# The first experts of a mixture-of-experts kernel: the order in which rows, tables and splits are asked for is changed

## The chip, the cores and the metric

The kernel runs on one core of a Trainium2 chip. The metric is the device time of one launch in microseconds (us); lower is better. The core has a matrix engine (TensorE, "PE" in the profile, with "PEld" for its weight loads), VectorE ("DVE"), ScalarE ("ACT"), GpSimd ("POOL"), and SyncE ("SP"), which here only issues transfers. Each engine works through its own list of instructions in the order in which the program gives them, and waits on counters (semaphores) that other engines and transfers raise.

## The reference

`x` is 32 x 128 x 1024 in float32, 4096 tokens of 1024. Two layers are added to it. Only the first matters here:

```
y      = each block of 128 tokens times one of 200 matrices (128 x 128)
probs  = softmax(y @ gate_w.T)                      # 64 experts
w, sel = top_k(probs, 8); w = w / sum(w)
inp[e] = the first 256 tokens that chose expert e   # a slot with no token counts as zero
h      = silu(inp[e] @ wg[e]) * (inp[e] @ wu[e])    # 1024 -> 384
out[e] = h @ wd[e]                                  # 384 -> 1024
x     += sum over a token's experts of w * out[e]
```

The second layer multiplies by a 1024 x 1024 matrix with low-rank additions; nothing in it is touched.

## The kernel before, in words

The kernel has three stages. The first (up to about 150 us) works out `y` and the routing, and stores in HBM `yd` (the rows of y), `wdr` (the routing weights), `tabd` (a table from which the tokens of each expert's slots are counted out) and `accd` (x, to which experts add). The second, which the change touches, goes through 64 experts. The third is the second layer.

**One expert on TensorE.** Weights and rows are split into a high and a low float32r part (HR and LR for weights, the two halves of XX for rows, hH and hL for h), and products are taken of the parts. `up(e)` makes three blocks, n = 3e, 3e+1, 3e+2, each of 32 matmuls (g, then u, with eight k each; lines 785 to 789), into two pairs of PSUM banks used in turn. So block n may begin only when VectorE has read block n-2: `if n >= 2: eng.wait_ge(s_gs, n - 1)`, and s_gs is raised by `join(n)`. `up(e)` also waits for the low part of all rows (`s_vl >= 2e+2`) and, unit by unit, for the weights (`s_L`). `down(e)` has 36 matmuls (line 802) in three groups j, each after hL of block 3e+j.

**A block after TensorE.** ScalarE copies half of it out (`copy_2`, L1089), VectorE adds the other half (`join`, L1522), ScalarE takes `silu` (L1093), VectorE multiplies (`product`, L1528), ScalarE rounds to hH (`high_h`, L1100), VectorE subtracts to hL (`low_h`, L1532).

**Weights.** An expert has six units of 768 KB (gA, gB, uA, uB, dA, dB), numbered through; SP loads them into four buffers `raw`. `split` is one instruction on ScalarE (HR, L1053, waiting for the load; for unit 6, which is gA of expert 1, also for stores of x) and one on VectorE (LR, L1486). The latter frees the buffer, so it releases the load of unit n+4.

**Rows.** GpSimd issues all indirect transfers, one instruction each, in a fixed order. `gather_x(e, c)` (L567) is four of them (a quarter of the columns of 128 slots each) into Xg[c]. For e >= 2 it waits for `index(e)` (s_i4) and for `turn_x(e-1, c)` (s_vt), which empties Xg[c]. `turn_x` is a VectorE transpose (L1504) from Xg[c] to XR[c]; `high_x` (ScalarE, L1081) and `low_x` (VectorE, L1510) then write XX.

**Tokens of an expert, two to three experts ahead.** `gather_tab(e)` (L542) is two transfers of 64 KB into G. `count(e)` and `token(e)` (VectorE, L1538 to L1548) wait for them and work out the slots' tokens; `spread(e)` (ScalarE, L1060 and L1064, seven small instructions) waits for `token(e)`; `index(e)` (VectorE, L1516) waits for `spread(e)`. `gather_w(e)` (L577) is two transfers of routing weights, `column(e)` (L1553) puts them in place (s_wc), `result` (ScalarE, L1107, four for one expert) scales by them, and `scatter` (L589) adds the result to accd. `gather_w(e)` waits for `column(e-2)`.

The order in which each engine does this is written out by hand: a prologue for expert 0 and the eve of expert 1, then a loop over e. In the loop, ScalarE does for e = 1: spread(3), the four results of expert 0, high_x(2, 0), high_x(2, 1), split dB 1, copy_2(3). VectorE, in the prologue: count(3), token(3), split dA 1; then in the loop turn_x(2, 0), turn_x(2, 1), index(3), low_x(2, 0), low_x(2, 1), join(3).

Of the kernel before, what the change touches and what calls it, by code (L numbers as in the profile page):

```python
# [16 lines left out]
E = 64  # L17
# [36 lines left out]
def adaln_ffn_kernel(nc, x, cond, adap, w0, gate_w, wg, wu, wd, W, A, Bm, scal,  # L54
# [14 lines left out]
    with ExitStack() as ctx:  # L69
# [437 lines left out]
        def _(eng):  # L507
# [26 lines left out]
            def gather_tab(e):  # L534
                if e == 2:
                    for s in range(4):
                        eng.wait_ge(d_ts[s], 16 * (NB // 4))
                    eng.wait_ge(s_idx, 1)
                if e >= 4:
                    eng.wait_ge(s_tok, 2 * (e - 1))  # L540
                for c in range(2):
                    eng.indirect_dma_start(G[:, e % 2, c, :], None, tab,  # L542
                                           bass.IndirectOffsetOnAxis(ap=rowi[:, c * E + e:c * E + e + 1], axis=0))\
                       .then_inc(d_g[e % 2], 16)
# [13 lines left out]
            def gather_x(e, c):  # L558
                if c == 0:
                    eng.wait_ge(s_i4, e)  # L560
                if e >= 2:
                    eng.wait_ge(s_vt, 2 * (e - 2) + c + 1)
                else:
                    eng.wait_ge(s_x0, 2 * c + 2)
                for q in range(4):
                    i = 2 * q + c
                    eng.indirect_dma_start(Xg[:, c, q, :], None, yd4,  # L567
                                           bass.IndirectOffsetOnAxis(ap=idx4[:, e % 4, i:i + 1], axis=0))\
                       .then_inc(d_xg[c], 16)

            def gather_w(e):
                if e >= 2:
                    eng.wait_ge(s_wc, e - 1)
                else:
                    eng.wait_ge(d_wy, 16 * NB // 4)
                for c in range(2):
                    eng.indirect_dma_start(Wg[:, e % 2, c, :], None, wdr,  # L577
                                           bass.IndirectOffsetOnAxis(ap=toki[:, c * E + e:c * E + e + 1], axis=0))\
                       .then_inc(d_wg[e % 2], 16)

            def scatter(e):
                if e >= 1:
                    eng.wait_ge(d_sc, 32 * e)
                else:
                    for s in range(2):
                        eng.wait_ge(d_ak[s], 16 * len(KEPT[s]))
                for c in range(2):
                    eng.wait_ge(s_out, 4 * e + 2 * c + 2)
                    eng.indirect_dma_start(acc, bass.IndirectOffsetOnAxis(ap=toki[:, c * E + e:c * E + e + 1], axis=0),  # L589
                                           ot[:, c, :], None, compute_op=ALU.add).then_inc(d_sc, 16)  # L590
# [2 lines left out]
            gather_x(1, 0)  # L593
            gather_tab(2)
            gather_x(1, 1)
            gather_tab(3)
            gather_w(0)
            gather_w(1)
            for e in range(E + 1):
                if 1 <= e < E - 3:  # L600
                    gather_tab(e + 3)
                if e >= 1:
                    scatter(e - 1)
                if e + 2 < E:
                    gather_x(e + 2, 0)
                    gather_x(e + 2, 1)
                    gather_w(e + 2)
# [346 lines left out]
        def _(eng):  # L954
# [57 lines left out]
            def store_w(i):  # L1012
                eng.wait_ge(s_wy, i + 1)
                a = i - 3
                eng.dma_start(wdr[a * P:(i + 1) * P, :].rearrange("(b q) e -> q b e", q=P),
                              wy[:, a:i + 1, :]).then_inc(d_wy, 16)
# [27 lines left out]
            def split(k, e):  # L1044
                n = pos[(k, e)]
                eng.wait_ge(d_raw[n % NRAW], 16 * (n // NRAW + 8))
                if n == 5:
                    eng.wait_ge(d_ak[0], 16 * len(KEPT[0]))
                if n == 6:
                    eng.wait_ge(d_ak[1], 16 * len(KEPT[1]))  # L1050
                if n >= NHL:
                    wait_retired(eng, n - NHL)
                eng.activation(HR[:, (n + 2) % NHL, :], raw[:, n % NRAW, :], ACT.Copy).then_inc(s_H, 1)  # L1053

            def spread(e):
                eng.wait_ge(s_tok, 2 * e + 2)
                if e >= 5:
                    eng.wait_ge(s_i4, e - 4)
                for q in range(4):
                    eng.activation(tq[0:32, e % 4, q, :], tokf[32 * q:32 * q + 32, e % 4, :], ACT.Copy)\  # L1060
                       .then_inc(s_tq, 1)
                eng.wait_ge(s_tq, 4 * e)
                for f in range(1, 4):
                    eng.activation(tq[32 * f:32 * f + 32, e % 4, :, :], tq[0:32, e % 4, :, :], ACT.Copy)\  # L1064
                       .then_inc(s_f, 1)
# [7 lines left out]
            def high_x(e, c):  # L1073
                eng.wait_ge(s_vt, 2 * (e - 1) + c + 1)
                if e == 1 and c == 0:
                    eng.wait_ge(d_wy, 16 * NB // 4)
                    for s in range(4):
                        eng.wait_ge(d_ts[s], 16 * (NB // 4))
                if e >= 2:
                    eng.wait_ge(s_up, 3 * (e - 1))  # L1080
                eng.activation(XX[:, e % 2, :, c * P:(c + 1) * P].rearrange("p j (q t) -> p q j t", q=4), XR[:, c, :, :, :],  # L1081
                               ACT.Copy).then_inc(s_vh, 1)
# [50 lines left out]
            for i in range(NB - 4, NB):  # L1133
                share(i)
            store_w(NB - 1)
            spread(1)
            split("uA", 0)
            for g in range(2):
                for c in range(2):
                    high_0(g, c)  # L1140
# [10 lines left out]
            spread(2)  # L1151
            high_x(1, 0)
            copy_2(2)
            high_x(1, 1)
            silu(2)
            high_h(2)
            for k in ("gA", "gB", "uA", "uB", "dA"):
                split(k, 1)
            for e in range(1, E):
                if e < E - 2:  # L1160
# [128 lines left out]
        def _(eng):  # L1289
# [189 lines left out]
            def split(k, e):  # L1479
                n = pos[(k, e)]  # L1480
                eng.wait_ge(s_H, n + 1)
                if n == 5:
                    eng.wait_ge(d_ak[0], 16 * len(KEPT[0]))
                if n == 6:
                    eng.wait_ge(d_ak[1], 16 * len(KEPT[1]))
                eng.tensor_tensor(LR[:, (n + 2) % NHL, :], raw[:, n % NRAW, :], HR[:, (n + 2) % NHL, :].bitcast(F32),  # L1486
                                  ALU.subtract).then_inc(s_L, 1)
# [67 lines left out]

            split("gA", 0)
            split("gB", 0)
            index(1)
            split("uA", 0)
            for g in range(2):  # L1560
                for c in range(2):
                    low_0(g, c)
# [14 lines left out]
            low_h(1)  # L1577
            turn_x(1, 0)
            index(2)
            turn_x(1, 1)  # L1580
            join(2)
            low_x(1, 0)
            product(2)
            low_h(2)
            low_x(1, 1)
            column(0)
            column(1)
            for k in ("gA", "gB", "uA", "uB"):
                split(k, 1)
            count(3)  # L1590
            token(3)
            split("dA", 1)
# [8 lines left out]
            for e in range(1, E):  # L1601
                if e < E - 1:
                    turn_x(e + 1, 0)
                    turn_x(e + 1, 1)
                    if e + 2 < E:
                        index(e + 2)
                    low_x(e + 1, 0)
                    low_x(e + 1, 1)
                join(3 * e)
                if e < E - 1:  # L1610
                    column(e + 1)
                product(3 * e)
                low_h(3 * e)
                split("dB", e)
                join(3 * e + 1)
                if e < E - 3:
                    count(e + 3)
                product(3 * e + 1)
                if e < E - 3:
                    token(e + 3)  # L1620
                low_h(3 * e + 1)
                if e + 1 < E:
                    split("gA", e + 1)
                else:
                    low_w(0)
                join(3 * e + 2)
                if e == E - 1:
                    eng.wait_ge(s_up, 3 * E)
                    eng.wait_ge(s_bh, 1)
                    eng.tensor_tensor(BL[:, :, D + NA:NX], laR[:, :, :, :].rearrange("p q a r -> p q (a r)"),  # L1630
                                      BH[:, :, D + NA:NX].bitcast(F32), ALU.subtract).then_inc(s_bl, 1)
                product(3 * e + 2)
                low_h(3 * e + 2)
                if e + 1 < E:
                    for k in ("uA", "gB", "uB", "dA"):
                        split(k, e + 1)
# [193 lines left out]
```

## Time and profile before

| what | value |
|---|---|
| median of 3 runs | 2403.81 us (2399.71 to 2403.9) |
| the profiled execution, its own time | 2391.3 us |
| its span, first to last instruction | 2389.5 us |
| busy: PE, DVE, ACT, POOL | 99%, 73%, 57%, 59% of the span |
| mean granted TensorE clock | 0.996 |

The profiled execution took 1.8 us beside its span, and was 12.5 us under the median of the runs. "Idle before" in a row is time in which that engine stood before the instruction, and the name behind it is what it waited for last. All positions are us from the span's start.

### The profile page before, as it was taken

Reading aid. Unit: us, or ns where it says so; the run is one execution under the profiler, and the core shown is the slowest. Engines: PE = TensorE matmul, PEld = TensorE weight load, DVE = VectorE, ACT = ScalarE, POOL = GpSimd, SP = SyncE. Lnnn points to the kernel's source line nnn. Section 1 sums busy time; section 2 is a strip of 40 time slices with the busy share of each in tenths; the row PEclk is TensorE's granted clock in tenths of the full one; section 3 lists DMA queues with packets and bytes.
Section 4 is the critical chain, followed back from the end, with each engine's and each line's share of the span. In section 5 each row is a group of like instructions: output and inputs, shape, how many; then the busy total and the mean of one; then the engine's idle time right before and its main releaser. Section 6 shows DMA issues by size and latency. Waiting matters only on the chain.

```text
span 2389.5 us, 35288 instructions
## 1 busy us (share of the span) xinstructions
PE 2355.3 (99%) x12762; PEld 2075.4 (87%) x12762; DVE 1734.9 (73%) x2874; ACT 1371.2 (57%) x2256; POOL 1409.5 (59%) x1032
## 2 busy tenths in 40 slices
PE   7988999999999999999999999999999999999999
PEld 5677888888888888888888888888889999999999
DVE  6887888888878878888888888887852255555554
ACT  5766777777767767777777776777751211111110
POOL 4028777787778777777777777777710132222221
PEclk9999999999999999999999999999999999999999
DMA  9998999899998998989989899899875354444441
GB/s 337 382 334 281 280 289 279 277 284 288 283 284 286 284 284 277 285 273 289 280 276 286 280 284 284 273 286 285 275 189 119 87 140 130 130 130 130 130 121 56
DMA packets 250352, 582.33 MB, mean 244 GB/s; under 512 B 82745, under 2 KB 106682, under 8 KB 250178
## 3 DMA queue, kind: packets, MB, share of 16 engines
q1 hardware_dynamic: 183202, 401.18, 51.2%
q0 software_dynamic: 55584, 160.02, 25.8%
q10 hardware_dynamic: 11392, 18.88, 2.1%
q8 instruction: 101, 1.65, 0.3%
q14 instruction: 73, 0.60, 0.1%
HBM read 456.51 MB, written 123.45 MB: 243 GB/s over the span
## 4 chain that ended last, share of the span: by engine, by line
PE 94%; DVE 1%; DMA 1%; POOL 1%; ACT 1%; issue 1%; ACTq 0%; SPq 0%; DVEq 0%; POOLq 0%
PE ps L789 26%; PE ps L802 22%; PE ps L898 16%; PE ps L788 13%; PE ps L856 5%; PE ps L785 4%; PE ps L658 2%; PE ps L891 2%; PE ps L786 2%; PE ps L668 1%; PE ps L871 1%; POOL Xg L567 1%; PE ps L681 0%; PE ps L680 0%; DMA bmR<-accd 0%
## 5 line engine op out<-in xcount | busy, mean ns | idle before, releaser
L789 PE MATMUL ps<-XX,HR 128*128 128x512 f32 x2688 | 961.6, 397 | 0.0
L788 PE MATMUL ps<-XX,LR 128*128 128x256 f32 x2688 | 751.5, 280 | 0.0
L567 POOL DMA_INDIRECT Xg<-yd,idx x504 | 654.0, 1298 | 158.5 <-issue 153.2
L1486 DVE TENSOR_TENSOR LR<-raw,HR 128x1536 fp32r<-128x1536 f32 x384 | 657.1, 1752 | 3.1 <-ACT HR L1053 3.1
L789 PEld LDWEIGHTS ps<-XX,HR 128*128 128x128 f32 x2688 | 506.2, 188 | 104.5
L1053 ACT ACTIVATE HR<-raw 128x1536 fp32r<-128x1536 f32 x384 | 556.6, 1479 | 11.9 <-DMA raw<-in_L_ffn_wd 10.3
L788 PEld LDWEIGHTS ps<-XX,LR 128*128 128x128 f32 x2688 | 508.5, 189 | 18.2 <-DVE LR L1486 0.6
L589 POOL DMA_INDIRECT accd<-ot,toki x128 | 255.9, 2000 | 159.5 <-ACT ot L1107 139.4
L898 PE MATMUL ps<-MH,xT 128*128 128x392 f32 x1536 | 335.9, 344 | 0.0
L802 PE MATMUL ps<-LR,hH 128*128 128x512 f32 x768 | 302.5, 394 | 0.0
L802 PE MATMUL ps<-HR,hL 128*128 128x512 f32 x768 | 301.1, 392 | 0.0
L802 PE MATMUL ps<-HR,hH 128*128 128x512 f32 x768 | 299.1, 389 | 1.3 <-DVE hL L1532 1.3
L898 PEld LDWEIGHTS ps<-MH,xT 128*128 128x128 f32 x1536 | 272.0, 188 | 2.3
L1522 DVE TENSOR_TENSOR gu<-ps,gu 128x512 f32<-128x512 f32 x192 | 132.7, 691 | 175.5 <-ACT gu L1089 175.5
L621 POOL DMA_INDIRECT m8a<-m8d,midx x32 | 27.7, 864 | 315.4 <-PE ps L871 314.8
L1089 ACT ACTIVATE gu<-ps 128x512 f32<-128x512 f32 x192 | 113.8, 593 | 159.4 <-PE ps L789 159.4
L542 POOL DMA_INDIRECT G<-tabd,rowi x124 | 166.2, 1340 | 39.0 <-issue 37.2
L577 POOL DMA_INDIRECT Wg<-wdr,toki x128 | 159.0, 1242 | 39.0 <-issue 38.7
L898 PE MATMUL ps<-ML,xT 128*128 128x392 f32 x768 | 181.1, 341 | 0.0
L802 PEld LDWEIGHTS ps<-HR,hL 128*128 128x128 f32 x768 | 144.2, 188 | 33.2
L802 PEld LDWEIGHTS ps<-HR,hH 128*128 128x128 f32 x768 | 144.2, 188 | 30.8 <-DVE hL L1532 1.7
L802 PEld LDWEIGHTS ps<-LR,hH 128*128 128x128 f32 x768 | 144.4, 188 | 28.7
(214 smaller groups left out, 3299.6 us busy)
## 6 DMA issues: line engine op xcount, KB each, us to landing
raw<-in_L_ffn_wd SPq DMA_DIRECT2D x128, 768.0 KB, 4.9
raw<-in_L_ffn_wg SPq DMA_DIRECT2D x126, 768.0 KB, 7.5
raw<-in_L_ffn_wu SPq DMA_DIRECT2D x126, 768.0 KB, 7.0
yd<-yrow ACTq DMA_DIRECT2D x32, 512.0 KB, 6.7
x<-accd SPq DMA_DIRECT2D x32, 512.0 KB, 5.2
out<-osb SPq DMA_DIRECT2D x31, 512.0 KB, 3.0
xt<-in_x SPq DMA_DIRECT2D x25, 512.0 KB, 8.0
accd<-xt SPq DMA_DIRECT2D x25, 512.0 KB, 6.4
```

Source lines behind the costliest of these rows:

```text
L542: eng.indirect_dma_start(G[:, e % 2, c, :], None, tab, bass.IndirectOffsetOnAxis(ap=rowi[:, c * E + e:c * E + e + 1], axis=0))\
L567: eng.indirect_dma_start(Xg[:, c, q, :], None, yd4, bass.IndirectOffsetOnAxis(ap=idx4[:, e % 4, i:i + 1], axis=0))\
L577: eng.indirect_dma_start(Wg[:, e % 2, c, :], None, wdr, bass.IndirectOffsetOnAxis(ap=toki[:, c * E + e:c * E + e + 1], axis=0))\
L589: eng.indirect_dma_start(acc, bass.IndirectOffsetOnAxis(ap=toki[:, c * E + e:c * E + e + 1], axis=0), ot[:, c, :], None, compute_op=ALU.ad ...
L788: eng.matmul(bank(out, 0, CAP), wl, xx[:, 0:CAP], start=False, stop=False)
L789: mm = eng.matmul(bank(out), wh, xx, start=False, stop=(k == 7))
L802: mm = eng.matmul(bank(4 + o), X[:, j, c * P:(c + 1) * P], Wt[:, s, j * 512:(j + 1) * 512], start=(j == 0 and m == 0), stop=(j == 2 and m ...
L856: mm = eng.matmul(bank(b0 + g, 0, z - a), X[:, j % 2, q, :], Y[:, q, a:z], start=(q == 0 and m == 0), stop=(q == 7 and m == 2))
L898: return eng.matmul(bank(lbank(t) + n, 0, 392), X[:, k, :], (MH, ML, MH)[m][:, k, a:a + 392], start=(k == 0 and m == 0), stop=(k == 7 and ...
L1053: eng.activation(HR[:, (n + 2) % NHL, :], raw[:, n % NRAW, :], ACT.Copy).then_inc(s_H, 1)
L1486: eng.tensor_tensor(LR[:, (n + 2) % NHL, :], raw[:, n % NRAW, :], HR[:, (n + 2) % NHL, :].bitcast(F32), ALU.subtract).then_inc(s_L, 1)
L1522: eng.tensor_tensor(gu[:, :, :], ps[:, b0:b0 + 2, 0:CAP], gu[:, :, :], ALU.add).then_inc(s_gs, 1)
```

## The change

It moves instructions in the prologue only, and removes and adds none.

- GpSimd: after gather_x(1, 1) the order was tab(3), w(0), w(1), x(2, 0), x(2, 1), w(2). It becomes w(0), x(2, 0), x(2, 1), tab(3), w(1), w(2). The loop then starts at e = 1 as before.
- ScalarE: split uA 0 ahead of spread(1); split gA 1 behind copy_2(2), ahead of silu(2); high_x(1, 1) behind high_h(2).
- VectorE: split uA 0 ahead of index(1); low_x(1, 0) ahead of join(2); turn_x(1, 1) behind low_h(2), then split gA 1, low_x(1, 1), the splits gB, uB and uA; column(0) behind those and ahead of count(3); column(1) between the two turns of expert 2.

```diff
--- before.py
+++ after.py
@@ -593,14 +593,16 @@
             gather_x(1, 0)
             gather_tab(2)
             gather_x(1, 1)
+            gather_w(0)
+            gather_x(2, 0)
+            gather_x(2, 1)
             gather_tab(3)
-            gather_w(0)
             gather_w(1)
-            for e in range(E + 1):
-                if 1 <= e < E - 3:
+            gather_w(2)
+            for e in range(1, E + 1):
+                if e < E - 3:
                     gather_tab(e + 3)
-                if e >= 1:
-                    scatter(e - 1)
+                scatter(e - 1)
                 if e + 2 < E:
                     gather_x(e + 2, 0)
                     gather_x(e + 2, 1)
@@ -1133,8 +1135,8 @@
             for i in range(NB - 4, NB):
                 share(i)
             store_w(NB - 1)
+            split("uA", 0)
             spread(1)
-            split("uA", 0)
             for g in range(2):
                 for c in range(2):
                     high_0(g, c)
@@ -1151,10 +1153,11 @@
             spread(2)
             high_x(1, 0)
             copy_2(2)
-            high_x(1, 1)
+            split("gA", 1)
             silu(2)
             high_h(2)
-            for k in ("gA", "gB", "uA", "uB", "dA"):
+            high_x(1, 1)
+            for k in ("gB", "uA", "uB", "dA"):
                 split(k, 1)
             for e in range(1, E):
                 if e < E - 2:
@@ -1555,8 +1558,8 @@
 
             split("gA", 0)
             split("gB", 0)
+            split("uA", 0)
             index(1)
-            split("uA", 0)
             for g in range(2):
                 for c in range(2):
                     low_0(g, c)
@@ -1577,16 +1580,16 @@
             low_h(1)
             turn_x(1, 0)
             index(2)
-            turn_x(1, 1)
+            low_x(1, 0)
             join(2)
-            low_x(1, 0)
             product(2)
             low_h(2)
+            turn_x(1, 1)
+            split("gA", 1)
             low_x(1, 1)
+            for k in ("gB", "uA", "uB"):
+                split(k, 1)
             column(0)
-            column(1)
-            for k in ("gA", "gB", "uA", "uB"):
-                split(k, 1)
             count(3)
             token(3)
             split("dA", 1)
@@ -1601,6 +1604,8 @@
             for e in range(1, E):
                 if e < E - 1:
                     turn_x(e + 1, 0)
+                    if e == 1:
+                        column(1)
                     turn_x(e + 1, 1)
                     if e + 2 < E:
                         index(e + 2)
```

## Rows read from the trace of the kernel before

**Rows 1.** The page's busy line: engine, us (share of the span), instructions.

```profile
PE 2355.3 (99%) x12762; PEld 2075.4 (87%) x12762; DVE 1734.9 (73%) x2874; ACT 1371.2 (57%) x2256; POOL 1409.5 (59%) x1032
```

**Rows 2.** TensorE waits from 150 us on: us in total, times, longest.

```profile
PE ps L785 <- DVE gu L1522: 5.2, 1, 5.2
...
PE ps L785 <- DVE XX L1493: 1.6, 1, 1.6
PE ps L802 <- DVE hL L1532: 1.3, 1, 1.3
...
PE ps L785 <- DVE LR L1486: 0.6, 1, 0.6
```

**Rows 3.** Chain that ended last, 155 to 232 us: start, us, what.

```profile
197.76 6.41 DMA Xg<-yd,idx
204.19 1.26 DVE XR L1504
...
208.41 0.70 DVE gu L1522
```

**Rows 4.** TensorE in order of time: start, us, line, operation [idle before].

```profile
209.16 0.79 PE L785 MATMUL ps<-XX,HR 128*128 128x512 f32 x1 [5.20 <-DVE gu L1522]
...
214.41 0.39 PE L785 MATMUL ps<-XX,HR 128*128 128x512 f32 x1
```

**Rows 5.** TensorE in stretches: A:B us, busy (instructions), granted clock, DMA, GB/s.

```profile
207.00:208.00 1.00, 0.00 (x0) 0.77 1.14 74
```

**Rows 6.** DVE, 148 to 245 us, in order of time; x2, x4 are merged.

```profile
159.68 1.76 DVE L1486 TENSOR_TENSOR LR<-raw,HR 128x1536 fp32r<-128x1536 f32 x1 [1.14 <-ACT HR L1053]
...
173.38 0.42 DVE L1532 TENSOR_TENSOR hL<-prod,hH 128x256 fp32r<-128x256 f32 x1 [0.48 <-ACT hH L1100]
...
181.39 0.32 DVE L1516 TENSOR_SCALAR idx<-tq,f 128x8 int32<-128x8 f32 x1
...
189.87 6.76 DVE L1486 TENSOR_TENSOR LR<-raw,HR 128x1536 fp32r<-128x1536 f32 x4
196.55 0.34 DVE L1538 TENSOR_SCALAR_CACHE_REDUCE Gj<-G,slot 128x128 f32<-128x128 f32 x1
```

**Rows 7.** ACT, 148 to 245 us, in order of time.

```profile
172.03 0.41 ACT L1093 ACTIVATE sil<-gu 128x256 f32<-128x256 f32 x1
...
182.46 0.58 ACT L1089 ACTIVATE gu<-ps 128x512 f32<-128x512 f32 x1
...
202.01 1.08 ACT L1081 ACTIVATE XX<-XR 128x1024 fp32r<-128x1024 f32 x1
205.47 1.06 ACT L1081 ACTIVATE XX<-XR 128x1024 fp32r<-128x1024 f32 x1 [2.38 <-DVE XR L1504]
```

**Rows 8.** SP's issues from 167 us.

```profile
167.27 0.96 SPq L367 DMA_DIRECT2D raw<-in_L_ffn_wg  x2
```

**Rows 9.** Transfers issued 167 to 167.6 us: count, KB each, us to landing.

```profile
raw<-in_L_ffn_wg SPq DMA_DIRECT2D x1, 768.0 KB, 16.0
```

**Rows 10.** DVE groups by shape, 180 to 210 us: busy, mean ns, idle before.

```profile
L1504 DVE STREAM_TRANSPOSE XR<-Xg 128x1024 f32<-128x1024 f32 x4 | 5.0, 1242 | 5.2 <-DMA Xg<-yd,idx 5.2
L1510 DVE TENSOR_TENSOR XX<-XR,XX 128x1024 fp32r<-128x1024 f32 x4 | 4.8, 1216 | 0.0
```

**Rows 11.** POOL, 148 to 245 us, in order of time.

```profile
179.51 0.94 POOL L542 DMA_INDIRECT G<-tabd,rowi  x1 [0.30 <-issue]
...
185.76 1.87 POOL L567 DMA_INDIRECT Xg<-yd,idx  x1 [0.30 <-issue]
...
192.75 1.36 POOL L567 DMA_INDIRECT Xg<-yd,idx  x1 [0.30 <-issue]
...
199.01 1.82 POOL L577 DMA_INDIRECT Wg<-wdr,toki  x1 [0.30 <-issue]
```

**Rows 12.** Transfers into G, 150 to 215 us: from issue to landing.

```profile
DMA to landing us min/median/max: 5.7/6.0/6.2
```

**Rows 13.** The same over the whole span, x124.

```profile
DMA to landing us min/median/max: 5.6/6.9/8.4
```

## The prediction

> **What bounds the kernel now.** I read the page first: TensorE is busy 99% of the span [rows 1], so almost only the places where it stands can be won. The list of its waits behind the routing stage gives those: 8.7 us lie around experts 0 and 1, the largest one wait of 5.2 us [rows 2]; between there and the end of expert 63 no wait of TensorE is listed. A microsecond won or lost at experts 0 and 1 therefore moves the end by a microsecond.
>
> The chain that ended last names the cause of the 5.2 us [rows 3]: the last quarter of expert 2's rows is asked for at 197.76 and lands 6.4 us later; its turn, its high and low parts and a split follow, then join(3), at 208.41. Only then may block 5 start, at 209.16; TensorE had stopped at 209.16 - 5.20 = 203.96 [rows 4]. The stall also costs clock: the granted clock falls within 207 to 208 us [rows 5], and the first 16 matmuls behind the stall take 214.41 - 209.16 = 5.25 us at the lower level (1.2 instead of 2.4 GHz), of which half, 2.6 us, is loss.
>
> The change reaches for this stall. So the question is when join(3) can run, and I follow each of its conditions.
>
> **The start (uA's split ahead of spread and index).** VectorE stood 1.14 us before this split, since ScalarE did spread(1) first [rows 6]. Now the wait goes, index(1) comes behind the split at about the time at which GpSimd is free for it anyway, and TensorE's wait of 1.6 us shrinks. Bounds 0 and 1.14 us, I take 0.6. Whether it reaches the end depends on the later stall; see the sum.
>
> **ScalarE's split gA 1 ahead of silu(2).** copy_2(2) ends at 182.46 + 0.58 = 183.04 [rows 7]. The load of gA 1 was issued at 167.27 and took 16.0 us [rows 8, 9], so it lands at 183.3: the split runs 183.3 to 184.7, and silu(2) is behind it. From silu to the end of low_h a block takes 1.77 us (172.03 to 173.38 + 0.42) [rows 6, 7], so hL is there at 186.5. TensorE waited for it until about 188.1; most of its 1.3 us goes.
>
> **VectorE's new order.** turn_x(1, 1) comes behind low_h(2): 186.5 + 1.2 = 187.7. Then split gA 1 (1.7, a quarter of the four that took 6.76) to 189.4 and low_x(1, 1) (1.2) to 190.5 [rows 6, 10]. up(1) can start at 190.6. Before, gA's split ended near 189.87 + 1.69 = 191.6 [rows 6] and set the start, so this is 1.1 us earlier. Blocks 3 and 4 are then paced by the next three splits, ending at 190.5 + 3 x 1.69 = 195.6 rather than 196.6. Block 4 ends about 202.8 instead of 203.96. So far the change gains 1.1 us, but only in reaching the next wait sooner.
>
> **GpSimd's new order.** x(2, 0) needs index(2), done at 181.7 [rows 6], so it starts at 182.0, not 185.76. x(2, 1) needs turn_x(1, 1), 187.7, and starts at 188.0. Issues follow each other every 1.25 us where nothing disturbs (0.94 + 0.30 at 179.51), every 1.66 us beside splits on VectorE (1.36 + 0.30 at 192.75), and over the eight row issues of before every (199.01 - 185.76) / 8 = 1.66 us [rows 11]. The second half of table 3 is the sixth issue from 188.0, five steps on: 6.25 us without disturbance, 8.3 by the mean. VectorE works through a split and a low part without a pause just then, and the first issues lose most behind such work, as the one at 185.76 did (1.87 us against 0.94). I take 9.5 us, so table 3's second half is asked for at 197.5 (bounds 194.2 and 198.0). In the old order it was asked for at 179.51.
>
> Expert 2's last rows now go out two issues ahead of that, at 195.0, and land near 195.0 + 6.4 = 201.4 instead of 204.2. The wait that the change attacks is therefore gained on by 2.8 us.
>
> **What is late next: table 3.** count(3) on VectorE needs both halves of it. It ran at 196.55 without any wait [rows 6]; VectorE will now reach it at about 195.7. The table's transfers take 5.7 to 6.2 us here [rows 12], 5.6 to 8.4 over the span [rows 13]. With 6.0 the table is there at 203.5, and VectorE stands almost 8 us. In its queue behind count(3) are token(3), split dA 1, both turns of expert 2, index(3), both low parts and join(3). ScalarE stands too: spread(3) waits for token(3), and behind it are the four results of expert 0, high_x(2, 0), high_x(2, 1), split dB 1 and copy_2(3), without which there is no join(3). How long this takes is in the trace: count(3) at 196.55 to high_x(2, 0) at 202.01 is 5.46 us of ScalarE working without a wait; the next high_x would have followed 1.0 us later; from high_x(2, 1) at 205.47 to TensorE at 209.16 are 3.69 us [rows 4, 6, 7]. Together 10.1 us. VectorE's own list is shorter (token, split, two turns, two low parts, about 9 us), so ScalarE's counts.
>
> Block 5 then starts at 203.5 + 0.1 + 10.1 = 213.7 instead of 209.16.
>
> The Trainium skill (DMA: Bandwidth & Descriptors, "Anatomy of one DMA — SWDGE (gpsimd) path") gives a GpSimd transfer about 2.0 us plus bytes / 436e3. Its rule would make 2.15 us of the table's 64 KB and start block 5 at 209.9, 0.7 us late only. The trace does not agree: not one of these transfers lands in under 5.6 us [rows 13].
>
> **The rest of the moves.** column(0) no longer waits and column(1) has its weights by its new place (asked for at 200.0 and 5 us on its way, needed past 207), so both cost their few tenths beside a standing engine. SP's queue: the release of gB 2's load hangs on split dA 1 and comes some 7 us later, but TensorE wants this unit only in expert 2, behind about 20 us; hidden. Expert 3's rows are behind scatter(0), which waits for the results: about 3 us later, while their need moves by 4.6 us; hidden. Clock: the stall is now 213.7 - 202.8 = 10.9 us long, the clock is down at its end as before, and I let the same 2.6 us stand (0.7 us either way).
>
> **Sum.** The 0.6 + 1.1 us won ahead of block 5 only lengthen the stall, since what ends it hangs on a landing and on GpSimd's list, not on TensorE. What counts is block 5: 213.7 - 209.16 = +4.6 us, all of which passes to the end. The profiled execution would take 2391.3 + 4.6 = 2395.9 us. The median of the runs is 12.5 us above that execution; laid on it, 2403.8 + 4.6 = 2408.4 us, +0.19%. A measurement of this kernel can tell about 0.2%, 4.8 us, from no change. Bounds of the unknown: table asked for at 194.2 and landed in 5.6 us gives block 5 at 210.0, +0.9 us; asked for at 198.0 and landed in 8.4 us gives 216.6, +7.4 us.
>
> **Rivals.**
> - *The table is late, but little.* GpSimd gets through its list at nearly 1.25 us an issue. Block 5 at 210.0 to 211.5, +0.9 to +2.3 us: 2405.5 us. For it: the issue at 179.51. Against: those beside the splits, 1.66 us and more [rows 11]. Chance 0.25.
> - *The other side: the rows decide and the stall shrinks.* Rows at 201.4 instead of 204.2 start block 5 at 206.4: -2.8 us, 2401.0 us; if the clock no longer falls, as it fell only some 4 us behind the stop [rows 5], up to 2.6 us more, 2398.4 us. It decides if the table is there by 206.4 - 10.1 = 196.3, so with 6.0 us on its way asked for by 190.3. That is 7 us ahead of what the issue rate gives. Chance 0.07.
> - *A second stall.* Expert 3's rows miss their turn, because GpSimd's list has slid and the scatter has slid into it. VectorE turned them with no wait before, and I find 1.6 us more room, so it needs an error of mine; a price of 2.5 us on top, 2410.9 us. Chance 0.08.
>
> **How the numbers follow.** My case (block 5 late by 2.5 to 7.4 us, through count(3)) has 0.60 and its own range is 2406 to 2411. The table case has 0.25, the faster one 0.07, the second stall 0.08. My case lies about the 4.8 us bound, so half of it is slower: slower 0.30 + 0.08, and a little for runs scattered upward, 0.40; same 0.52; faster 0.08. The range of 2401 to 2413 takes in both bounds, the faster rival without clock and the second stall.
>
> **What would show it.** Right: TensorE's waits list one of about 11 us at L785 for join(3); VectorE has a new wait of about 8 us for G before L1538 of count(3) at about 203.5; ScalarE stands as long before L1060; waits for Xg at L1504 vanish; the wait of 1.3 us at L802 is gone or short; up(1) begins near 190.6; no wait behind 230 us. Wrong: table 3 issued ahead of about 194 us, or G landing in 3 us, or count(3) no longer the head of both queues; or a gain ahead of block 5 that reaches the end.

## The result, and the profile after

The changed kernel takes 2406.72 us (median of 16 runs, 2403.89 to 2411.34) beside 2403.57 us (2399.71 to 2411.55) for the kernel before in the same comparison: ratio 1.0016, 95% interval 1.0009 to 1.0023. That is +3.15 us by the medians, +2.2 to +5.5 us by the interval: a little slower; the median difference is within the 0.2% that was called "same", the upper end of the interval is just beyond it. The prediction was 2408.4 us, +4.6.

The profiled execution took 2407.89 us by its own time, its span is 2406.1 us. This is 16.6 us longer than the span of before, and most of it is not the change. The first gather of expert 0's rows, which ends the routing stage, was issued at 153.14 in the profiled execution of before and is here at 164.99; in a second execution of the kernel before it is at 165.48. The 11.85 us between the two lie ahead of everything that the change moves. They go with the granted clock of the first 50 us: 1.00 in the profile of before and in the three others of this document whose first gather is at 152 to 155 us, 0.86 to 0.90 in the ten whose first gather is at 163 to 165 us. Kernels with and without the change stand in both groups. From here on I count positions from this gather and call it T0.

TensorE's waits of after from 150 us on (total, times, longest), against [rows 2]:

```profile
PE ps L787 <- DVE gu L1525: 10.8, 1, 10.8
PE ps L804 <- DVE hL L1535: 2.7, 1, 2.7
...
PE ps L787 <- DVE XX L1496: 1.0, 1, 1.0
```

The one wait of 5.2 us for join(3) has become one of 10.8. The other two went two ways: the start's from 1.6 to 1.0, that for hL from 1.3 up to 2.7. (TensorE's and ScalarE's lines stand 2 further down than before, VectorE's 3.)

TensorE of after in order of time; the first row is block 0, the second the last of the three groups of down(0), the third block 5, the last the 17th matmul of block 5, as in [rows 4]:

```profile
173.92 0.50 PE L787 MATMUL ps<-XX,HR 128*128 128x512 f32 x1 [0.98 <-DVE XX L1496]
...
199.16 0.50 PE L804 MATMUL ps<-HR,hH 128*128 128x512 f32 x1 [2.69 <-DVE hL L1535]
...
226.21 0.80 PE L787 MATMUL ps<-XX,HR 128*128 128x512 f32 x1 [10.83 <-DVE gu L1525]
...
231.19 0.39 PE L787 MATMUL ps<-XX,HR 128*128 128x512 f32 x1
```

Why join(3) is late stands on VectorE, in order of time:

```profile
202.96 5.09 DVE L1489 TENSOR_TENSOR LR<-raw,HR 128x1536 fp32r<-128x1536 f32 x3
207.96 0.16 DVE L1556 COPY wcol<-Wg 128x2 f32<-128x2 f32 x1
216.21 0.35 DVE L1541 TENSOR_SCALAR_CACHE_REDUCE Gj<-G,slot 128x128 f32<-128x128 f32 x1 [8.09 <-DMA G<-tabd,rowi]
...
225.46 0.69 DVE L1525 TENSOR_TENSOR gu<-ps,gu 128x512 f32<-128x512 f32 x1 [0.44 <-ACT gu L1091]
```

VectorE has done its splits and column(0), and then stands 8.09 us at count(3), for a table that arrives at 216.2. In [rows 6] the same instruction had no wait at all. From count(3) to block 5 are 226.21 - 216.21 = 10.0 us, the list that the prediction put at 10.1. ScalarE is empty meanwhile:

```profile
195.95 1.49 ACT L1055 ACTIVATE HR<-raw 128x1536 fp32r<-128x1536 f32 x1 [1.18 <-DMA raw<-in_L_ffn_wg]
...
217.65 0.88 ACT L1062 ACTIVATE tq<-tokf 32x2 f32<-32x2 f32 x4 [9.87 <-issue]
219.25 2.42 ACT L1109 ACTIVATE ot<-ps,wcol 128x512 f32<-128x512 f32 x4
221.55 2.02 ACT L1083 ACTIVATE XX<-XR 128x1024 fp32r<-128x1024 f32 x2
```

It stands 9.87 us ahead of spread(3); results, both high_x and copy_2(3) follow. And GpSimd shows when the table was asked for:

```profile
164.99 0.96 POOL L554 DMA_INDIRECT Xg<-yd,toki  x1 [78.80 <-DVE toki L1464]
...
193.94 0.94 POOL L567 DMA_INDIRECT Xg<-yd,idx  x1 [1.74 <-DVE idx L1519]
...
200.53 2.19 POOL L567 DMA_INDIRECT Xg<-yd,idx  x1 [1.51 <-DVE XR L1507]
203.03 2.50 POOL L567 DMA_INDIRECT Xg<-yd,idx  x1 [0.30 <-issue]
205.83 1.37 POOL L567 DMA_INDIRECT Xg<-yd,idx  x1 [0.30 <-issue]
207.50 1.37 POOL L567 DMA_INDIRECT Xg<-yd,idx  x1 [0.30 <-issue]
...
210.43 0.94 POOL L542 DMA_INDIRECT G<-tabd,rowi  x1 [0.30 <-issue]
```

x(2, 1), the rows from 200.53 on, had to wait for turn_x(1, 1), which the change put behind low_h(2); then its four issues took 7.4 us beside the splits. The table's second half went out at 210.43, T0 + 45.4; before it was T0 + 26.4 (179.51 - 153.14).

### The profile page after: what moved, and what is told of

It reads as the page before. It is cut to its first block, busy times and chain, and to the rows that moved or that the text cites. A ratio compares the mean times of both kernels' runs of the same rounds, so it can differ in the third digit from the quotient of the medians.

```text
span 2406.1 us, 35288 instructions
## 1 busy us (share of the span) xinstructions
PE 2358.3 (98%) x12762; PEld 2076.3 (86%) x12762; DVE 1735.6 (72%) x2874; ACT 1370.5 (57%) x2256; POOL 1408.0 (59%) x1032
## 4 chain that ended last, share of the span: by engine, by line
PE 95%; DMA 1%; DVE 1%; issue 1%; ACT 1%; another core or an unknown queue 0%; SPq 0%; ACTq 0%; POOL 0%; DVEq 0%; POOLq 0%
PE ps L791 25%; PE ps L804 21%; PE ps L900 17%; PE ps L790 13%; PE ps L858 5%; PE ps L787 4%; PE ps L660 2%; PE ps L893 2%; PE ps L788 2%; PE ps L670 1%; PE ps L873 1%; DMA raw<-in_L_ffn_wg 1%; PE ps L683 1%; PE ps L682 0%
```

## The experiments

All positions in this table are from T0, in us. "Rows" is the last request for expert 2's rows, "table" that for the second half of table 3.

| run | rows | table | count(3) | join(3) | down(1) | ratio to before (95%) |
|---|---|---|---|---|---|---|
| before | 44.6 | 26.4 | 43.4 | 55.3 | 64.1 | 1 |
| b_again | 43.0 | 26.3 | 43.5 | 54.6 | 62.0 | 1.0002 (0.9991, 1.0013) |
| after | 42.5 | 45.4 | 51.2 | 60.5 | 69.0 | 1.0016 (1.0009, 1.0023) |
| after_again | 42.8 | 45.7 | 51.7 | 60.9 | 70.1 | 1.0023 (1.0014, 1.0032) |
| tab_ahead | 43.4 | 26.6 | 42.2 | 54.4 | 63.6 | 0.9993 (0.9983, 1.0004) |
| count_later | 42.7 | 46.2 | 55.0 | 54.3 | 62.8 | 0.9988 (0.9977, 0.9999) |
| gp_only | 37.4 | 40.7 | 47.9 | 57.1 | 63.6 | 1.0003 (0.9993, 1.0014) |
| eng_only | 45.8 | 26.4 | 43.4 | 56.9 | 65.6 | 0.9997 (0.9988, 1.0006) |
| gp_count_later | 38.4 | 41.7 | 51.4 | 50.7 | 57.1 | 0.9982 (0.9973, 0.9991) |
| join_first | 44.6 | 26.3 | 43.4 | 46.4 | 56.8 | 0.9977 (0.9968, 0.9986) |
| join_first_again | 44.3 | 27.3 | 44.8 | 52.8 | 63.0 | 0.9987 (0.9977, 0.9997) |
| all_fixed | 45.4 | 38.0 | 44.4 | 47.4 | 57.0 | 1.0006 (0.9997, 1.0015) |
| all_fixed2 | 43.7 | 35.5 | 42.6 | 45.5 | 55.8 | 0.9984 (0.9975, 0.9993) |
| join_first2 | 44.4 | 26.0 | 43.2 | 46.2 | 56.3 | 0.9985 (0.9975, 0.9994) |

**The kernel before, again (b_again).** No edit: what one profiled execution can tell from another.

> The kernel before once more, for a second profile and for the spread. All theories: ratio 1.000, within 0.001. If the 11.9 us that the profile of the changed kernel shows more than that of before by the end of the routing stage belong to single executions and not to the change, this profile may show them too (span near 2401); if it comes out near 2389.5 again, the change would have to answer for them. In either case TensorE's wait for join(3) should be about 5 us.

The median is 2401.85 beside 2401.89 us: no difference. T0 is 165.48, so the 12 us of the routing stage belong to the execution and not to a kernel. The 5.2 us wait, though, isn't there. TensorE's rows show gaps in block 4 for which the profile names no releaser, and a lower clock right behind them, and the block ends 1.1 us after join(3) was done:

```profile
213.51 0.28 PE L788 MATMUL ps<-XX,LR 128*128 128x256 f32 x1 [0.24 <-issue]
214.97 0.39 PE L789 MATMUL ps<-XX,HR 128*128 128x512 f32 x1 [0.81 <-issue]
216.41 0.37 PE L788 MATMUL ps<-XX,LR 128*128 128x256 f32 x1 [0.70 <-issue]
```

Block 5 begins at T0 + 56.4, where it began at 56.0 in the other execution, so nearly the same microseconds are lost. Whether this is the same stall in another form isn't shown: by its rows TensorE was still in block 4 when join(3) ended. The list of waits alone is thus no safe measure; join(3)'s own position (55.3 and 54.6) is what two executions agree on, to 0.7 us, and I judge by it.

**The table asked for ahead of expert 2's rows (tab_ahead).** The change with this one thing taken back; column(1) goes behind join(3), since its weights come later.

```diff
+            gather_tab(3)
             gather_w(0)
             gather_x(2, 0)
             gather_x(2, 1)
-            gather_tab(3)
...
                     turn_x(e + 1, 0)
-                    if e == 1:
-                        column(1)
```

> The changed kernel with table 3 asked for ahead of expert 2's rows again (the weights of expert 0 and the rows behind it), and column(1) behind join(3), since its weights now come last. My theory (the table's late landing is the whole of the loss): count(3) runs without a wait near where VectorE reaches it, the rows decide, block 5 starts about 2.2 us earlier than in the kernel before and 7 us earlier than in the changed one, counted from the first rows' gather; time 2401.4 us, ratio 0.999; with a clock that stays up some 2.5 us less, ratio 0.998. Rival (the order of the splits or the gathers costs something else): ratio 1.001 as the changed kernel.

count(3) is back at 42.2 without a wait, join(3) at 54.4, some 6 us ahead of the change and 0.2 to 0.9 ahead of before. The ratio is below that of the change by 0.0023, about 5.5 us. The table's place is the whole loss, as far as the runs can tell. What it doesn't show is the gain that I had given the rows: block 5 is at T0 + 55.2, 0.8 us ahead of before and not 2.2, and VectorE again waits for them, as before.

```profile
208.90 1.24 DVE L1507 STREAM_TRANSPOSE XR<-Xg 128x1024 f32<-128x1024 f32 x1
213.91 1.25 DVE L1507 STREAM_TRANSPOSE XR<-Xg 128x1024 f32<-128x1024 f32 x1 [3.77 <-DMA Xg<-yd,idx]
218.14 0.69 DVE L1525 TENSOR_TENSOR gu<-ps,gu 128x512 f32<-128x512 f32 x1 [0.53 <-ACT gu L1091]
```

**The table late, but out of the way (count_later).** GpSimd's order stays as changed; count(3) and token(3) go behind join(3), index(3) behind low_h(3), spread(3) behind high_h(3), and column(1) behind join(3).

```diff
-            count(3)
-            token(3)
             split("dA", 1)
...
                 join(3 * e)
+                if e == 1:
+                    column(1)
+                    count(3)
+                    token(3)
...
```

> The changed kernel with everything of expert 3's table (count, token, spread, index) and column(1) moved behind join(3); GpSimd's order is that of the change, so the table is asked for as late as there. My theory: the table's late landing no longer matters, the rows of expert 2 decide and land about 2.8 us earlier than in the kernel before, so block 5 starts 2.8 us earlier than before; time 2400.8 us, ratio 0.999 (0.998 if the clock stays up); expert 3's rows are asked for some 3 us later than before and should just be in time. Rival (GpSimd's new order is bad in itself, by the transfers' traffic or by the issue rate): ratio 1.001 or more.

The table is asked for as late as in the change, at 46.2, but nothing of block 3 stands behind it: join(3) at 54.3, ratio 0.9988. Block 5 is at 55.0, 1.0 us ahead of before and not the 2.8 that I had expected of the rows. With the two runs together the cause is shown from both sides: it is neither the late table by itself nor the place of count(3), but that count(3) stands in the queue ahead of join(3) while the table is on its way.

**GpSimd's order alone (gp_only) and the two other engines' alone (eng_only).** gp_only is the kernel before with the changed order of gathers, and column(1) between the turns of expert 2; eng_only is the reverse.

```diff
-            gather_tab(3)
             gather_w(0)
-            gather_w(1)
-            for e in range(E + 1):
+            gather_x(2, 0)
+            gather_x(2, 1)
+            gather_tab(3)
+            gather_w(1)
+            gather_w(2)
+            for e in range(1, E + 1):
...
```

> The kernel before with GpSimd's new order alone, and column(1) between the turns as in the change (ahead of the splits it would stand for weights that now come last). My theory: x(2, 1) is not held by the late turn, so the table is asked for about 2 us earlier than in the changed kernel; count(3) still waits, some 5 us; block 5 starts about 2.4 us later than in the kernel before; ratio 1.001. Rival (the moves on VectorE and ScalarE make the loss): ratio 0.999, since the rows come earlier.

> The kernel before with the moves on VectorE and ScalarE alone; GpSimd keeps the old order. My theory: up(1) starts about 1 us earlier, count(3) does not wait, but expert 2's last rows are asked for about when they were (GpSimd's list is the same, and the turn that it waits for is done at about 34 to 35 us behind the first rows' gather, when x(2, 1) would not be issued before 37 to 38 anyway), so join(3) stays near 54.5 to 55.3 us behind that gather; ratio 1.000. Rival (the engines' moves make the loss): join(3) later by 2 us or more, ratio 1.001 or more.

In gp_only the rows are asked for by 37.4, 5 us ahead of the change: turn_x(1, 1) stands in its old place, so x(2, 1) is free early, and seven of its eight issues take 0.95 to 1.02 us each. The last two on GpSimd:

```profile
198.88 0.95 POOL L567 DMA_INDIRECT Xg<-yd,idx  x1 [0.30 <-issue]
200.14 1.36 POOL L567 DMA_INDIRECT Xg<-yd,idx  x1 [0.30 <-issue]
```

In spite of that join(3) is at 57.1, 1.8 to 2.5 us behind before, since count(3) waited 4.9 us for the table. The time is unchanged (1.0003). In eng_only x(2, 1) is not held by the turn, which ends at 190.3 while the first issue of x(2, 1) comes at 195.84, right behind the one before it. What is late are the issues themselves: the last two of x(2, 0) and the first of x(2, 1) fall beside a low part and splits:

```profile
190.24 2.50 POOL L567 DMA_INDIRECT Xg<-yd,idx  x1 [0.30 <-issue]
193.04 2.50 POOL L567 DMA_INDIRECT Xg<-yd,idx  x1 [0.30 <-issue]
195.84 1.36 POOL L567 DMA_INDIRECT Xg<-yd,idx  x1 [0.30 <-issue]
```

The last request is at 45.8 and join(3) at 56.9, 1.6 to 2.3 us behind before, where I had expected it to stay; its time too is not told from no change (0.9997). So each half puts join(3) back by about 2 us, which the times don't show, and together they put it back by 5 to 6. The rest beyond the two halves comes through x(2, 1), behind which GpSimd's part has put the table. Against gp_only x(2, 1) starts 1.9 us later in the change (35.5 against 33.6), as the engines' part delays turn_x(1, 1), and from its first to its last issue it takes 7.0 us instead of 3.8, as it now runs beside the splits.

**Both handicaps gone (gp_count_later).** gp_only with count(3), token(3), spread(3) and index(3) behind block 3, as in count_later.

> GpSimd's new order with the turns of the kernel before, and expert 3's table (count, token, spread, index) and column(1) behind join(3). Expert 2's last rows should be asked for near 37.4 us behind the first rows' gather, as with GpSimd's new order alone, 5 us earlier than in the changed kernel, since the turn they wait for is not moved back and fewer of the issues stand beside splits. My theory: with the table out of the way join(3) then comes at 51 to 52 us, limited by the lists and no more by rows; down(1) at 57.5 to 59. A second wait at block 8 as in all_fixed is likely and takes 1 to 3 us back; ratio 0.998. Rival (rows asked for earlier win nothing, whatever the table does): join(3) at 54 us or later, ratio 0.999 to 1.000.

Join(3) is at 50.7, 3.6 us ahead of count_later, and TensorE's wait ahead of block 5 is down to 1.8 us:

```profile
215.44 0.50 PE L787 MATMUL ps<-XX,HR 128*128 128x512 f32 x1 [1.80 <-DVE gu L1526]
```

The ratio is 0.9982, 4.3 us under before. So asking early for expert 2's rows goes with an earlier join(3), if the turn stays where it was and the table's consumers are out of the way. How much of the time is due to the rows isn't shown: count_later, with rows at 42.7 instead of 38.4, has 0.9988, and the two intervals overlap. The second wait at block 8 that I had thought likely did not come (0.35 us).

**Block 3 worked off first (join_first, join_first_again).** The kernel before, in which only the work on block 3 goes ahead of expert 2's turns, results and high parts, of none of which it needs anything.

```diff
             for e in range(1, E):
+                if e == 1:
+                    join(3)
+                    product(3)
+                    low_h(3)
                 if e < E - 1:
                     turn_x(e + 1, 0)
```

and so for copy_2(3), silu(3) and high_h(3) on ScalarE; their old places are left out for e = 1.

> The kernel before, in which for expert 1 alone block 3 is worked off at once: copy_2(3), join(3), silu, product, high_h and low_h ahead of the turns and parts of expert 2's rows, which up(2) needs only 17 us later. GpSimd's order is that of before. My theory: what holds TensorE is only that join(3) stands in both lists behind work that it does not need. Then the wait of 5 us and its clock loss of up to 2.6 us go, and down(1) starts 7 us earlier (about 55 to 57 us behind the first rows' gather instead of 62 to 64); time about 2395 us, ratio 0.997. Rival (the stall comes back at down(1), since dB's split or hL is late in turn): ratio 0.999 or more.

> join_first once more on another occasion: down(1) at about 56.8 us behind the first rows' gather, no wait of TensorE at block 5, ratio 0.9977 within 0.001. If the gain was one of that occasion, 0.999 or more.

The first time join(3) is at 46.4, the stall at block 5 is gone, and the ratio is 0.9977, 4.7 us under before. VectorE goes from join(3) over product and low part to the turns, at 202.58 and 204.77, with 0.94 us left of the wait for rows:

```profile
199.95 0.68 DVE L1528 TENSOR_TENSOR gu<-ps,gu 128x512 f32<-128x512 f32 x1
202.58 1.24 DVE L1510 STREAM_TRANSPOSE XR<-Xg 128x1024 f32<-128x1024 f32 x1
204.77 1.25 DVE L1510 STREAM_TRANSPOSE XR<-Xg 128x1024 f32<-128x1024 f32 x1 [0.94 <-DMA Xg<-yd,idx]
```

The second time the same kernel has 0.9987, and the profiled execution (2401.24 us, beside a median of 2398.38) missed both positions that I had expected: join(3) is at 52.8, block 5 had a wait of 0.79 us, and down(1) began at 63.0 instead of 56.8. It shows what the new order can cost. TensorE began up(1) 2.7 us later than in join_first, VectorE stood 4.87 us at join(3) with expert 2's turns and the split of expert 1's dB behind it, and TensorE then waited for that split:

```profile
199.84 0.50 PE L802 MATMUL ps<-HR,hH 128*128 128x512 f32 x1 [2.40 <-DVE hL L1538]
216.40 0.50 PE L785 MATMUL ps<-XX,HR 128*128 128x512 f32 x1 [0.79 <-DVE gu L1528]
...
225.88 0.80 PE L802 MATMUL ps<-HR,hH 128*128 128x512 f32 x1 [3.60 <-DVE LR L1492]
```

Why join(3) was so late is open. VectorE waited for copy_2(3) on ScalarE, which began only at 215.03, although TensorE's rows have block 4 beginning at 209.86; the profile doesn't name what released it:

```profile
215.03 0.60 ACT L1089 ACTIVATE gu<-ps 128x512 f32<-128x512 f32 x1 [6.03 <-remote]
```

**All of it together (all_fixed), and the next block too (all_fixed2, join_first2).** all_fixed is the change with block 3 worked off first, and the table between x(2, 0) and x(2, 1). all_fixed2 and join_first2 are all_fixed and join_first with block 6 also worked off early, between the turns of expert 3 on VectorE and between its high parts on ScalarE:

```diff
                 if e < E - 1:
                     turn_x(e + 1, 0)
+                    if e == 2:
+                        join(6)
+                        product(6)
+                        low_h(6)
                     turn_x(e + 1, 1)
```

> The changed kernel with the same treatment of block 3 and with table 3 asked for between the two halves of expert 2's rows, where GpSimd otherwise waits for the turn; column(1) behind the low parts. My theory: as join_first, and 1 us more since up(1) starts earlier; time about 2394 us, ratio 0.9965. Rival (up(1)'s earlier start is used up by the splits, or by transfers of gA that land late): the same as join_first.

> all_fixed, in which for expert 2 as well block 6 is worked off early, between the two turns of expert 3's rows. In all_fixed TensorE reached down(1) 7 us earlier than in the kernel before, but stood 4.3 us at block 8 for join(6), which was queued behind expert 3's last rows. My theory: that second wait and the clock it cost are all that separates all_fixed from join_first; it goes, and the ratio is 0.997 to 0.998. Rival (the second wait only moves on, to up(3), since GpSimd's list has not become shorter): ratio 0.9995 or more.

> join_first, with block 6 worked off between the two turns of expert 3's rows (as in all_fixed2). My theory: the 0.4 us that TensorE still waited at block 8 goes, and the half microsecond is too small to measure: ratio 0.9975. Rival (block 6 this early takes ScalarE's and VectorE's time away from the rows and splits of expert 3): TensorE waits at down(2) or up(3), ratio 0.9985 or more.

all_fixed gained nothing (1.0006, where I had expected 0.9965), although join(3) was at 47.4. The stall had gone one expert further on. TensorE's list of waits and VectorE's row, where expert 3's rows come late and join(6) is behind them:

```profile
PE ps L787 <- DVE gu L1531: 4.3, 1, 4.3
```

```profile
229.42 1.25 DVE L1513 STREAM_TRANSPOSE XR<-Xg 128x1024 f32<-128x1024 f32 x1 [3.21 <-DMA Xg<-yd,idx]
```

So down(2) begins at T0 + 90.7, behind the 89.1 of before. With join(6) out of the way it begins at 83.3, and all_fixed2 has 0.9984. join_first2, at 0.9985 where I had expected 0.9975, isn't told from join_first's 0.9977 and 0.9987: where the rows of expert 3 are in time, the second edit buys nothing that shows.

**The change again (after_again).** The kernel after, measured together with all_fixed2 and gp_count_later.

> The changed kernel once more, for a second profile and a second comparison. All theories: ratio 1.0016 within 0.001. If the late table is the cause, count(3) again stands about 8 us for G, join(3) comes 60 to 61 us behind the first rows' gather (55.3 and 54.6 in two profiles of the kernel before), and down(1) 67.5 to 69 us (64.1 and 62.0 before). If instead the first profile was an odd execution, join(3) is nearer to 56.

2405.32 beside 2401.03 us, 1.0023, with join(3) at 60.9, block 5 at 61.7 and a wait of 10.2 us ahead of it; down(1) is at 70.1, 1 us behind what I had expected. The mechanism is the same.

Versions faster than both kernels, each with an interval below 1, are thus join_first (0.9977 and 0.9987), gp_count_later (0.9982), all_fixed2 (0.9984), join_first2 (0.9985) and, barely, count_later (0.9988); their intervals overlap, and I can't rank them.

## Why the prediction was right

**The mechanism held, to the places.** Block 5 was put 4.6 us later; it is at T0 + 61.2 instead of T0 + 56.0, 5.2 us later. The wait was put at 10.9 us and is 10.8, VectorE's at count(3) at almost 8 and is 8.09, the list from count(3) to block 5 at 10.1 and is 10.0. tab_ahead and count_later take the effect away, each in its own way. That the length of TensorE's wait agrees to 0.1 us is partly luck: it was put from 202.8 to 213.7 and runs, on the axis of before, from 203.5 to 214.4, so both ends are late by 0.7.

**The table's request.** Predicted at 197.5; on the axis of before (11.85 us less) it is 198.6, 1.1 us later. Of the 9.5 us that I gave six issues from turn_x(1, 1) on, 9.9 were needed (200.53 to 210.43); the rest is the turn, which was late. Landing took 5.8 us where I had 6.0.

**The start** went as put: 1.6 to 1.0 us.

**Wrong: the wait for hL, and up(1) 1.1 us earlier.** TensorE comes to this wait at 199.16 - 2.69 = 196.47, on the axis of before 184.6, where before it came at 188.11 - 1.30 = 186.8. Of these 2.2 us, 0.6 are the shorter wait at the start, and the rest lies in the clock: behind the 1.6 us of before the granted clock fell, behind the 0.98 us of after it did not. The same stretch of block 0 in before and in after:

```profile
164.00:166.00 2.00, 2.00 (x8) 0.50 0.97 216
```

```profile
174.00:176.00 2.00, 2.00 (x12) 1.00 1.01 336
```

The prediction had no clock term for the start. That the shorter wait kept the clock up isn't shown, though: other executions contradict it (last section). hL, on the other hand, came only 0.8 us sooner: the load of gA 1 landed at 195.95, on the axis of before 184.1 rather than 183.3, ScalarE waited 1.18 us for it, and silu(2) was behind. So the wait grew to 2.7 us, and behind this one the clock fell (last section). What was won at the start was lost here, and up(1) begins at 203.62, on the axis of before 191.77: exactly where it began in the trace of before, and not at 190.6. In the end none of it counts, as the stall of 10.8 us lies behind it.

**Put too high: rows 2.8 us sooner.** The last request was put at 195.0 and came at 195.6 on the axis of before (T0 + 42.5). That is 2.1 us ahead of the profiled execution of before but only 0.5 ahead of b_again: x(2, 1) has to wait for the turn that the same change put back, and is then issued beside splits. It is why tab_ahead brings join(3) only to 54.4. The faster rival of the prediction would have come to little even with the table in time.

**The second stall** did not come in the change, as its chance of 0.08 said, but all_fixed has it, at 4.3 us. The room for expert 3's rows is thus shorter than I put it, once TensorE runs ahead.

**The size.** +4.6 us was put, +3.15 (2.2 to 5.5) and +4.3 measured, while block 5 itself moved by 5.2. Single profiles scatter by more than the difference: down(1) is at 64.1 and 62.0 in two executions of before, at 69.0 and 70.1 in two of the change. Where the last microsecond or two went is not settled.

## What to carry over

When a transfer is moved back in one queue, look for its consumer in the other engines' queues: what counts is not when that consumer is needed, but what stands behind it, here 10 us of work for block 3 that needed nothing of the table. Work that frees the bound engine goes ahead of work that waits for a transfer, but with a second look at the splits and turns that then stand behind it, and at the next expert, where the same stall can return. And a change made of several moves should be taken apart, and its parts judged by positions too: two halves whose times showed no difference had each put join(3) back by 2 us, and together they made a loss.

## What the hardware showed that I had not expected

**GpSimd's issues beside VectorE.** With no VectorE instruction that reads two tensors in SBUF beside it (a split, a low part, a product), the issue of an indirect transfer (rows, tables or weights) took 0.94 to 1.02 us, in all 170 cases up to 246 us in the 14 profiles. With one beside it 434 issues took 0.94 to 2.57 us, 219 of them 1.3 us or more. In the change the issue at 203.03 took 2.50 us with splits beside it, and after the last of them, which ends at 208.05, an issue is back at 0.94. The Trainium skill (SBUF — State Buffer, "SBUF: two separate sides") says that VectorE and GpSimd share a pair of ports under an exclusive lock, which a VectorE instruction with two SBUF inputs holds for its whole length against a GpSimd operation that reads SBUF. The rows agree as far as the inputs go: the turns read one tensor and take about as long as a low part (1.24 us beside 1.21), and none of the 34 issues that had a turn but no two-input instruction beside it took over 0.95 us. That it is the port itself isn't shown, and many issues beside a two-input instruction are not slowed.

**Short waits can cost clock.** After a wait of 2.5 us ahead of the last group of down(0) the granted clock fell to the lower level for the next 3 us. join_first2 in stretches (TensorE busy, granted clock, DMA, GB/s), and its first matmuls behind the wait:

```profile
199.00:202.00 3.00, 3.00 (x8) 0.50 0.56 193
```

```profile
198.74 0.66 PE L802 MATMUL ps<-HR,hH 128*128 128x512 f32 x1 [2.52 <-DVE hL L1542]
199.19 0.63 PE L802 MATMUL ps<-HR,hL 128*128 128x512 f32 x1
```

Eight steps from one matmul to the next take 0.43 us instead of 0.23, a loss of 1.6 us. The clock fell in the same way behind this wait in eight other profiles, among them the change (2.69 us), tab_ahead (1.98), count_later (2.86), gp_only (3.13) and eng_only (2.97), and in before behind the 1.6 us at the start; ahead of the same group of down(0) it did not behind waits of 0.82 (gp_count_later), 0.86 (b_again), 1.08 (join_first) and 1.30 us (before). So a wait of TensorE can cost more than its own length, unless a later stall hides it. But the length of the wait doesn't settle it. At the start of expert 0 join_first2 waited 1.60 us, as before did, and kept the clock, and all_fixed waited 0.98 us, as the change did, and lost it; join_first2 and then all_fixed, each for the 4 us behind that wait:

```profile
173.70:177.70 4.00, 4.00 (x23) 1.00 0.94 311
```

```profile
162.30:166.30 4.00, 4.00 (x15) 0.60 1.03 351
```

With the changed order of the start the clock stayed up in six of seven profiles, with the old one in two of seven; what decides is open. So the 2.2 us that the change won at the start are a difference of two executions, and no price of the wait. Behind the long stall of the change the clock had fallen too, and stayed at the lower level into block 5:

```profile
222.00:226.00 4.00, 0.00 (x0) 0.50 0.89 188
226.00:230.00 4.00, 3.79 (x12) 0.50 1.04 221
...
231.00:234.00 3.00, 3.00 (x19) 1.00 0.87 324
```

The 16 matmuls of this stretch took 4.98 us, those of before 5.25 [rows 4]: a stall of twice the length cost no more clock.
